# One product pair instead of 22 per block to spread routing weights in a GRU, attention and mixture-of-experts layer

## What is computed

```python
def cell(h, x):                          # 512 times, one after the other
    gi, gh = x @ W_ih + b_ih, h @ W_hh + b_hh
    r = sigmoid(i_r + h_r); z = sigmoid(i_z + h_z)
    n = tanh(i_n + r * h_n)
    return (1 - z) * n + z * h
scores = sigmoid(hs @ gate_w.T)          # tokens x 16
topv, topi = top_k(scores, 2)            # two experts per token
dw = zeros(T, E).at[rows, topi].add(topv / topv.sum(-1))
y = (silu(hs @ sw1.T) * (hs @ sw3.T)) @ sw2.T          # shared, 704 units
for e in range(16):                      # each expert, every token
    y = y + dw[:, e] * ((silu(hs @ w1[e].T) * (hs @ w3[e].T)) @ w2[e].T)
out = x + y
```

## Time and profile before

| | |
|---|---|
| median of three runs | 2664.43 us (2659.36 to 2669.05) |
| the profiled execution | 2660.29 us, span 2658.4 us |
| PE busy | 2534.4 us, 95% |
| PEld busy | 1986.8 us, 75% |
| VectorE busy | 1875.2 us, 71% |
| GpSimd busy | 1126.7 us, 42% |
| ScalarE busy | 1061.8 us, 40% |
| weight products L1310 | 352 matmuls |
| copies L1048 | 176, 101.6 us |
| scan starts, block 1 starts, tail starts | 575.2, 829.5, about 2503 us |

### The profile page before, as it was taken

The page is one execution under the profiler, slowest core; times in us unless marked ns, Lnnn a source line. Parts: engine busy times, 40 slices in busy tenths (PEclk is TensorE's granted clock), DMA queues, the critical chain, the costliest instruction groups (busy, mean ns, idle before and its releaser), DMA issues.

```text
span 2658.4 us, 159495 instructions
## 1 busy us (share of the span) xinstructions
PE 2534.4 (95%) x69538; PEld 1986.8 (75%) x69538; DVE 1875.2 (71%) x7064; ACT 1061.8 (40%) x3613; POOL 1126.7 (42%) x2952
## 2 busy tenths in 40 slices
PE   7788987879999999999999999999999999999999
PEld 3334343458887888888888888888888888888888
DVE  5656666546667787887778787778777877778622
ACT  5465554443333333333333333333333333333333
POOL 3313121013333555455455545545554555455454
PEclk9899999999999999999999999999999999999999
DMA  4100000010112333333233333323332333232244
GB/s 174 41 18 18 18 2 2 2 34 30 50 50 68 98 95 98 95 93 101 85 104 95 93 95 95 99 84 99 95 94 87 109 93 97 87 92 88 91 147 132
DMA packets 146187, 209.41 MB, mean 79 GB/s; under 512 B 16464, under 2 KB 86352, under 8 KB 145232
## 3 DMA queue, kind: packets, MB, share of 16 engines
q1 hardware_dynamic: 144336, 195.01, 23.6%
q10 hardware_dynamic: 1152, 4.19, 0.4%
HBM read 185.51 MB, written 13.63 MB: 75 GB/s over the span
## 4 chain that ended last, share of the span: by engine, by line
PE 72%; DVE 3%; POOL 1%; issue 1%; ACT 1%; DMA 0%; DVEq 0%; POOLq 0%; ACTq 0%
PE ps L1286 27%; PE ps L1321 25%; PE ps L1336 12%; PE ps L1298 6%; PE ps L1310 2%; POOL hidf L978 1%; DVE turn_n L1167 0%; DVE fresh L1180 0%; DVE turn L1170 0%; DVE hcur L1182 0%; DVE hcur L1185 0%; DVE npre L1173 0%; DMA w<-in_w 0%; ACT cand L1074 0%; DVE h L1183 0%
## 5 line engine op out<-in xcount | busy, mean ns | idle before, releaser
L1286 PE MATMUL ps<-whh,hcur 128*32 128x128 f16 x49152 | 789.4, 220 | 22.7 <-DVE hcur L1185 11.7
L1286 PEld LDWEIGHTS ps<-whh,hcur 128*32 128x32 f16 x49152 | 694.7, 97 | 142.8 <-DVE hcur L1185 119.3
L1321 PE MATMUL ps<-hb,w 128*128 128x256 f16 x6400 | 782.1, 273 | 0.7 <-DMA w<-in_w 0.7
L1321 PEld LDWEIGHTS ps<-hb,w 128*128 128x128 bf16 x6400 | 602.6, 98 | 96.8 <-DMA w<-in_w 1.4
L970 POOL COPY hb<-hcur 128x32 f16<-128x32 f16 x512 | 169.8, 332 | 663.2 <-DVE hcur L1185 663.2
L1067 ACT ACTIVATE r<-ur 128x16 f32<-128x16 f32 x512 | 110.6, 216 | 826.9 <-DVE ur L1161 826.9
L1336 PE MATMUL ps<-hid,w 128*128 128x256 f16 x3200 | 428.4, 273 | 2.2 <-POOL hid L990 1.8
L1336 PEld LDWEIGHTS ps<-hid,w 128*128 128x128 bf16 x3200 | 312.3, 98 | 39.7 <-issue 3.0
L978 POOL TENSOR_TENSOR hidf<-up 128x256 f32<-128x256 f32 x400 | 291.8, 730 | 97.9 <-POOL hid L990 50.1
L990 POOL TENSOR_TENSOR hid<-hidf,hid 128x256 f16<-128x256 f32 x400 | 268.8, 672 | 62.7 <-ACT hid L1063 62.7
L1158 DVE STREAM_TRANSPOSE turn<-ps 128x128 f32<-128x128 f32 x512 | 161.8, 316 | 180.3 <-PE ps L1286 171.0
(11 more groups left out here) (162 smaller groups left out, 3037.6 us busy)
## 6 DMA issues: line engine op xcount, KB each, us to landing
w<-in_w SPq DMA_DIRECT2D x400, 256.0 KB, 2.7
w<-in_w SPq DMA_DIRECT2D x400, 128.0 KB, 2.7
gi_scratch<-gis SPq DMA_DIRECT2D x72, 128.0 KB, 1.7
spare<-gi_scratch SPq DMA_DIRECT2D x36, 128.0 KB, 2.7
gi<-gi_scratch SPq DMA_DIRECT2D x36, 128.0 KB, 2.8
x2T<-in_xT SPq DMA_DIRECT2D x4, 1024.0 KB, 7.4
out<-xo ACTq DMA_DIRECT2D x8, 512.0 KB, 4.2
stage<-in_W_hh SPq DMA_DIRECT2D x3, 1024.0 KB, 5.4
```

The lines of the kernel that those rows point to most:

```text
L1286: mm = pe.matmul(ps[j * COLS:(j + 1) * COLS, bank, 0:P], hcur[:, k], whh[:, s, k, at:at + P], start=(k + s == 0), stop=(k == KT - 1 and s ...
L1321: mm = pe.matmul(ps[:, UB[u], w * TOK:(w + 1) * TOK], w13[:, u, w, k], hb[:, f % 2, s, k].rearrange("p b t -> p (b t)"), start=(w + k + s ...
```

## The change

The hidden units of the experts are dealt out to chunks in another order. A chunk now holds 16 rows (EACH) of each of eight experts. There are two kinds (KINDS) of chunk: 22 hold rows of experts 0 to 7 and 22 rows of experts 8 to 15, alternating. All chunks of a kind have the same owner matrix, so one pair of products per block, at step 9 as before, and one copy spread the weights for all 44 chunks. The rest of the pairs with their copies and waits is gone, the planner's formula no longer counts them, and the host side permutes w1, w3 and w2 alike. Owner and wsb get smaller.

```diff
-NWG = (NCH - SCH) // 2
+KINDS = 2
+EACH = P * KINDS // E
...
-        WEIGH = [GATE[SCH + 2 * p] - 1 for p in range(NWG)]
+        WEIGH = GATE[SCH] - 1
...
-            shares = sum(1 for at in WEIGH if EXPERTS <= at <= i)
-            total = UP * NCH - UPS[EXPERTS - 1] + DOWN * NCH - LATE + NWG - 1
-            downs = -(-total * (i - EXPERTS + 1) // (TB - EXPERTS)) - (UPS[i] - UPS[EXPERTS - 1]) - shares
+            total = UP * NCH - UPS[EXPERTS - 1] + DOWN * NCH - LATE
+            downs = -(-total * (i - EXPERTS + 1) // (TB - EXPERTS)) - (UPS[i] - UPS[EXPERTS - 1])
...
-            def share(f, p):
-                n = f * NWG + p
-                act.wait_ge(weighed, n + 1)
-                act.wait_ge(up2_done, f * NCH + SCH + 2 * (p - 1))
-                nc.scalar.copy(wsb[:, (p + SCH // 2) % 2], ps[:, WB, :]).then_inc(wsb_done, 1)
+            def share(f):
+                act.wait_ge(weighed, f + 1)
+                need(act, up2_done, f * NCH)
+                nc.scalar.copy(wsb[:].rearrange("p c t -> p (c t)"), ps[:, WB, :]).then_inc(wsb_done, 1)
...
-                    dve.wait_ge(wsb_done, f * NWG + (c - SCH) // 2 + 1)
-                    nc.vector.tensor_tensor(up2[:], ps[:, UB[c % 2], TOK:2 * TOK], wsb[:, (c // 2) % 2, (c % 2) * TOK:(c % 2 + 1) * TOK],
+                    dve.wait_ge(wsb_done, f + 1)
+                    nc.vector.tensor_tensor(up2[:], ps[:, UB[c % 2], TOK:2 * TOK], wsb[:, (c - SCH) % KINDS],
                                             ALU.mult).then_inc(up2_done, 1)
...
-            def weigh(f, p):
-                if p == 0:
-                    pe.wait_ge(dwT_hi, f + 1)
-                    pe.wait_ge(dwT_lo, f + 1)
-                need(pe, wsb_done, f * NWG + p)
-                for c in range(2):
-                    mm = pe.matmul(ps[:, WB, c * TOK:(c + 1) * TOK], owner[:, 2 * p + c], dwT[:],
+            def weigh(f):
+                pe.wait_ge(dwT_hi, f + 1)
+                pe.wait_ge(dwT_lo, f + 1)
+                for c in range(KINDS):
+                    mm = pe.matmul(ps[:, WB, c * TOK:(c + 1) * TOK], owner[:, c], dwT[:],
                                    start=(c == 0), stop=True, skip_group_check=True)
                 mm.then_inc(weighed, 1)
...
-                need(pe, wsb_done, f * NWG)
+                need(pe, wsb_done, f)
...
-                    for p in weigh_at[i]:
-                        weigh(f, p)
+                    if i == WEIGH:
+                        weigh(f)
...
-                if c >= SCH and c % 2 == 0:
-                    weigh(f, (c - SCH) // 2)
+                if c == SCH:
+                    weigh(f)
...
-        shared, own = np.asarray(sw), np.asarray(w).reshape(E * TOPI, D)
+        shared, own = np.asarray(sw), np.asarray(w).reshape(KINDS, E // KINDS, -1, EACH, D).transpose(2, 0, 1, 3, 4).reshape(E * TOPI, D)
...
-    owner = np.zeros((P, E * TOPI), w13.dtype)
+    owner = np.zeros((P, KINDS * P), w13.dtype)
     for e in range(E):
-        owner[e, e * TOPI:(e + 1) * TOPI] = 1
+        owner[e, e * EACH:(e + 1) * EACH] = 1
```

More of the change, by code:

```diff
@@ L816, in scan_and_ffn @@
         w2 = sb("w2", [P, W2S, D], BF16)
-        owner = sb("owner", [P, NCH - SCH, P], BF16)
+        owner = sb("owner", [P, KINDS, P], BF16)
         dwT = sb("dwT", [P, TOK], F16)
-        wsb = sb("wsb", [P, 2, 2 * TOK], F32)
+        wsb = sb("wsb", [P, KINDS, TOK], F32)
         sg = sb("sg", [P, 2, TOK], F32)
@@ L883, in scan_and_ffn @@
         GATE = [2, 3, 4, 6, 7, 8] + [EXPERTS + n * (TB - EXPERTS) // (NCH - SCH) for n in range(NCH - SCH)]
-        WEIGH = [GATE[SCH + 2 * p] - 1 for p in range(NWG)]
+        WEIGH = GATE[SCH] - 1
         gate_at = [[c for c in range(NCH) if GATE[c] == i] for i in range(TB)]
-        weigh_at = [[p for p in range(NWG) if WEIGH[p] == i] for i in range(TB)]
         LEFT = [4, 3, 4, 4, 3, 5, 4, 3, 2]
@@ L1110, in _ @@
                             sigmoid(f, c)
-                        for p in weigh_at[i]:
-                            share(f, p)
+                        if i == WEIGH:
+                            share(f)
                     if g + 1 < S:
@@ L1117, in _ @@
             for c in range(NCH):
-                if c >= SCH and c % 2 == 0:
-                    share(f, (c - SCH) // 2)
+                if c == SCH:
+                    share(f)
                 sigmoid(f, c)
@@ L1465 @@
         "gate": rows(np.asarray(L0_ffn_gate_w).T[unit]),
-        "w13": w13, "w2": w2, "owner": owner.reshape(P, NCH - SCH, P),
+        "w13": w13, "w2": w2, "owner": owner.reshape(P, KINDS, P),
         "ident": np.eye(P, dtype=np.float16),
```

## The result

The changed kernel takes 2642.81 us in the median of four runs (2640.66 to 2645.35), the kernel before 2663.94: a ratio of 0.9917 (95% interval 0.9905 to 0.9929), 21.1 us less. The same two kernels on another occasion gave 2648.54 and 2663.49, 0.9944 (0.9928 to 0.9961), 15.0 us less. The prediction was 2639 in a range of 2623 to 2652, from a sum of 22.6 us.

A forecast was written before the change was run, and what follows sets the result against it. PE was taken to bound fuller steps, the recurrence's loop (about 3.63 us) the rest. Scan 18.4 plus tail 4.2 made 22.6 us, giving 2637.7 from the profiled execution or 2641.8 from the median; forecast 2639, range 2623 to 2652.

The forecast's parts named there:

- What bounds the kernel: Scan steps: PE sets those above about 19 wide matmuls; below, the recurrence's own loop is a floor near 3.63 us.
- Counts: Steps 10 to 63 of a block: 22 with 20 wide matmuls, 32 with 18; L1310 16 times, L1048 8 times.
- Scan, 18.4 us: Blocks 1 to 7: 147 steps go from 3.743 to 3.63 us, 16.6 us, plus 1.8 for short steps behind short ones.
- blocks 1 to 7 each 2.4 to 2.9 us shorter: Sign for the scan: each of these blocks would take 2.4 to 2.9 us less than in the kernel before.
- The middle value for one short step behind another: Blocks 1 to 7: 70 nine-unit steps behind another, taken midway between 3.59 and 3.62 us, 1.8 us gained.
- rival 1: Scan steps: the floor gives way and the removed matmuls' full 36.7 us come, 2623.6 us; 5%.
- rival 2: Scan: the floor rises in runs of short steps, costing the whole 0.11 us; only the tail's 4.2 is left, 2656; 8%.
- Tail, 4.2 us: Feed-forward of block 7 alone: 21 weight pairs leave, 4.6 us, less 0.4 for slow up-weight loads.
- this sign (below 1 us): Sign for the tail: waits for w stay below 1 us.
- ScalarE, moved downs, waits at nothing: 168 fewer ScalarE copies, downs sliding by one step, and changed waits were each priced at 0 us.
- Rival 3: PE's instruction supply: "issue" pauses before narrow matmuls grow; 17 more of 1.3 us cancel the gain, 24 more give 2672; 5%.
- rival 4: Scan: nine-unit steps hide no late state, so perhaps 5 us of the gain is lost, 2644; 12%.

The follow-up runs named there:

- after_again: The changed kernel measured again on another occasion, with no edit: 2648.54 us, ratio 0.9944 to the kernel before.
- products_twice: The kernel before with each weight pair's two matmuls done twice: 2698.49 us, ratio 1.0131 to the kernel before.
- half-downs kernel: The changed kernel without the down work's matmuls for the low half of the hidden rows: 2601.19 us (two runs), ratio 0.9758 to the kernel before.
- after_small_loads: The changed kernel with expert weight loads cut to 64 KB a chunk instead of 384: 2626.63 us, ratio 0.9858 to the kernel before.

## Why the prediction was right, and where it wasn't

**What bounds the kernel.** Right in both halves. Above 18 wide matmuls PE sets the step (3.96, 3.743 and 3.634 us for 22, 20 and 19); below, the recurrence's loop does, and with the loop cut the step of 18 falls to the 3.525 that was worked out from the tail's price.

**Counts.** Right: the trace has 20 and 18 wide matmuls where the formulas put them, and L1306 ran 16 times, L1046 8 times. PE's share, which was to fall, is 95% on both pages.

**Scan, 18.4 us.** Right as a step-by-step sum (18.0 with the disturbance taken out). In the kernel as it is the blocks lost 8.0 and 11.5 us in two pairs of traces, and the sign "blocks 1 to 7 each 2.4 to 2.9 us shorter" failed: in the first pair they differ by 1.5 us the wrong way (block 2) to 3.9. With the loads cut each is 2.2 to 3.2 us shorter. The middle value for one short step behind another, 3.605, was fair: their medians in three traces are 3.580, 3.588 and 3.621. The floor neither gave way (rival 1) nor rose (rival 2).

**Tail, 4.2 us.** 4.2 and 5.3 in the two pairs. PE does meet late loads, as was allowed for: over the whole tail its loads wait for w 1.4 us in 4 times in the changed kernel and 0.2 once in after_again, beside 0.5 once and 0.9 twice in the kernel before's two traces. The 1.4 was over the limit set for this sign (below 1 us), and without these waits the tails would differ by 5.1 and 4.6 us.

**ScalarE, moved downs, waits at nothing.** Right; keeping the copies and keeping the old plan each left the time where it was. The gain of 2.3 us in block 0, which runs the same instructions in both kernels, was not forecast. All of it lies in the scan's second and third step. In the second the kernel before has a pause of 0.8 us at 582.0 us. In the third TensorE's granted clock stands at 0.50, the 1.2 GHz level, for 3.4 us, and the step takes 5.56 us where it takes 3.96 in the changed kernel. In the second step TensorE had mostly waited for the state in both (busy 1.71 of 4.00 us in the one, 1.52 of 3.50 in the other). The stretch tables of the two, the kernel before first:

```profile
584.90:588.30 3.40, 3.40 (x77) 2.70 (x64) 2.21 (x10) 0.75 (x4) 1.50 (x5) 0.50 0.00 0
```

```profile
583.80:587.20 3.40, 3.40 (x94) 2.86 (x86) 2.42 (x11) 1.23 (x5) 1.78 (x6) 1.00 0.02 5
```

Over the study's fourteen traces block 0 takes 251.6 to 254.5 us. The stretch at 0.50 is there in nine, the four of the kernel before and its cut forms among them, and costs 1.6 us in each; the four of the changed kernel and the same cut forms don't have it, nor has products_twice, but five other forms of the changed kernel do. Why the clock falls in some and not in others stays open.

**Pauses: the step that failed.** The sum has no term for pauses. Rival 3 named them and got 5%, because twice as many seemed too much for 1.3% more density; rival 4 put a loss of 5 us down to lateness of the state. The pauses did double, which was also a sign of being wrong, from 21 to 41 by the waits and from 10 to 20 us by the gaps, in each of two traces. They were not numerous enough to make the kernel slower, and not each 1.3 us long: 0.42 us is their mean (20.1 / 48). The density was priced over a whole step, 62.0 against 62.8 instructions a us, and that average doesn't decide. Lateness of the state, rival 4's reason, took little: with the loads cut the blocks are 18.0 us apart, 0.4 below the sum. The loss of some 10 us explains why the measured gain is below the sum: 22.6 - 10 is 12.6, beside 14.9 in the profiled pair (which has the 2.3 of block 0) and 15.0 in the second pair of medians. The first pair's 21.1 us is nearer to the sum than the pauses of its own profiled execution allow. That execution, 2645.35, is the highest of its four times, and there is no trace of the others. That the forecast of 2639 lies so near to 2642.81 is in part luck: the sum misses 10 us of pauses, block 0 gives back 2.3 that it didn't have, and the other occasion's 2648.54 is 6 us further off.

What is shown about the pauses is that they need the weight traffic, that they belong to a program and that short steps go with them: 24 to 32 where a block has 11 to 13 steps under 3.65 us, 43 to 63 where it has 27 and more. Whether it is the shorter step, the smaller number of wide matmuls in it or the places at which the instruction stream is cut is not told apart; the half-downs kernel, with the lightest steps of all, has no more of them (45) than the changed one.

## What to carry to other kernels

Price an edit per step, not per instruction: find the step length at which another chain takes over (here 3.625 us, at 18.9 wide matmuls), because work added costs its full price and work removed is paid only down to that floor. When work has been removed down to a floor, look at how the rest is spread; evening 20 and 18 to 19 gave another 8 to 13 us at no cost in instructions. And when a shortened step feeds an engine with thousands of small instructions, count its "issue" pauses in more than one trace of before and of after, as they repeat with the program and can eat half the gain.

## What the runs showed of the hardware

PE's pauses are late instruction fetches, as far as traces can show it. Two pauses in a row in the changed kernel:

```profile
874.10 0.57 PEld L1284 LDWEIGHTS ps<-whh,hcur 128*32 128x32 f16 x40 [0.21 <-DVE hcur L1183]
874.93 0.82 PEld L1284 LDWEIGHTS ps<-whh,hcur 128*32 128x32 f16 x56 [0.26 <-issue]
875.85 1.21 PEld L1317 LDWEIGHTS ps<-hb,w 128*128 128x128 bf16 x12
877.07 0.64 PEld L1332 LDWEIGHTS ps<-hid,w 128*128 128x128 bf16 x6
877.97 0.78 PEld L1284 LDWEIGHTS ps<-whh,hcur 128*32 128x32 f16 x53 [0.26 <-DVE hcur L1183]
879.11 0.62 PEld L1284 LDWEIGHTS ps<-whh,hcur 128*32 128x32 f16 x43 [0.36 <-issue]
```

```profile
q8 instruction: 544, 8.91, 1.4%
```

From pause to pause PE loads 56 + 12 + 6 + 53 = 127 weights, each with its matmul: 254 instructions. Other pauses are 127 loads or a near multiple apart. The page's instruction queue moves 8.91 MB in 544 packets, 16 KB each. The kernel before moves 547 of them for 69538 loads, this one 544 for 69202: 127 a packet in both. In the DMA records the last such packet before a pause's end lands 1.2 to 1.7 us ahead of it (median 1.41 in this kernel, 1.43 in the kernel before; of all narrow loads only a fifth to a quarter stand at such a distance). And the number of packets landed says where PE stops: at a pause's end PE has gone through 123 + 127.12 n loads, n being the packets landed by then, to within about one load for all 48 pauses of this kernel and three for the 24 of the kernel before.

The same line tells how near the other boundaries are. Counted from a packet's landing, PE comes to its first load after 1.72 and 1.76 us in the changed kernel's two traces (medians of the blocks), after 1.89 and 1.78 in the kernel before, and after 2.02 in after_small_loads. The packets' own time in the records is the same with the weight traffic cut (median 1.04 us), but they start earlier, 0.81 instead of 1.14 us after PE has passed the boundary before. So half of the boundaries have a reserve of some 0.3 us over the 1.4 at which PE pauses, and the weight traffic takes 0.3 from it. What holds a packet's start back is not in the records.

The Trainium skill's page "Runtime: NRT & Kernel Launch", section "Instruction fetch mechanics", says that instructions are refilled in blocks of 16 KiB, 256 instructions, and that crossing a block's boundary is mostly hidden. The trace agrees with the size. It also agrees that most crossings are hidden, but of the 393 to 409 packets that land in the blocks of these kernels with full loads 24 to 63 cost a pause, 10 to 29 us a run.

The recurrence's loop is itself not one number: a step of 18 wide matmuls or fewer takes 3.625 us behind one that PE fills, and 3.58 or 3.625 behind one that it doesn't. Which of the two it is goes with VectorE's work for the chunks (L1150 and L1152 in the changed kernel, here counted together). In after_half_downs, where no step is filled, the pause-free steps 11 to 62 have a median of 3.581 us where two of these instructions started in the step before (193 steps) and 3.625 where one did (109). In the changed kernel's steps behind a step of 18 it is 3.583 and 3.625. Why is not shown.
